# Attention scores from two float32r parts instead of three bf16 parts

## What is computed

```python
# first attention: 16 heads, 8 key heads, 32 numbers a head
q = q * cos + _rotate_half(q) * sin
k = k * cos + _rotate_half(k) * sin
att = jnp.einsum('bhqd,bhkd->bhqk', q, k) * scale
att = SOFTCAP * jnp.tanh(att / SOFTCAP)          # SOFTCAP = 50
att = jnp.where(causal[None, None], att, -jnp.inf)
att = jax.nn.softmax(att, axis=-1)
y = jnp.einsum('bhqk,bhkd->bhqd', att, v)
return y.transpose(0, 2, 1, 3).reshape(b, t, NH * HD) @ Wo
...
# second attention: 16 heads, 4 key heads, 16 numbers a head, no softcap
scores = jnp.einsum('bhqd,bhkd->bhqk', q, k) * scale
scores = jnp.where(causal[None, None], scores, jnp.finfo(scores.dtype).min)
attn = jax.nn.softmax(scores, axis=-1)
```

## Time and profile before

| | us |
|---|---|
| median of 3 runs | 3083.39 (3082.63 to 3088.0) |
| the profiled execution | 3089.23, of which the span from first to last instruction 3087.3 |
| `pa` with its norm, from the start | to 125 |
| `aa` | 125 to 453 |
| `pb` with its norm | 603 to 667 |
| `ab` | 667 to 1062 |
| PE, DVE, ACT, POOL busy over the whole span | 81%, 68%, 60%, 28% |

### The profile page before, as it was taken

How to read it: one execution, slowest core, us unless ns; L and a number is a source line. 1 busy time by engine, 2 the same in 40 slices (tenths; PEclk the granted TensorE clock), 3 DMA queues, 4 the chain that set the end, 5 groups by cost and what they waited for, 6 DMA issues and landing times. The chain is left out here.

```text
span 3087.3 us, 69834 instructions
## 1 busy us (share of the span) xinstructions
PE 2494.2 (81%) x25745; PEld 1664.7 (54%) x25832; DVE 2105.2 (68%) x4897; ACT 1849.8 (60%) x3604; POOL 873.3 (28%) x907
## 2 busy tenths in 40 slices
PE   7788877878888698577677677776999686899998
PEld 3333325643343385344444344445888565788888
DVE  7478886668787567599799899985333254666652
ACT  3388874324444443289799799993222332576678
POOL 2233334120000131255455455540000122223223
PEclk9899997878999898799999899998999776898999
DMA  3523312254233212512211222004000565522210
GB/s 123 140 47 66 70 23 91 87 108 56 45 38 42 71 52 98 108 21 29 30 16 14 30 29 29 1 1 169 1 1 1 104 137 96 127 39 33 31 41 11
DMA packets 291483, 174.00 MB, mean 56 GB/s; under 512 B 206416, under 2 KB 252512, under 8 KB 289120
## 3 DMA queue, kind: packets, MB, share of 16 engines
q1 hardware_dynamic: 282000, 161.40, 25.4%
q10 hardware_dynamic: 9168, 8.41, 1.0%
HBM read 113.84 MB, written 51.51 MB: 54 GB/s over the span
## 5 line engine op out<-in xcount | busy, mean ns | idle before, releaser
L1279 ACT ACTIVATE ad_e<-ps,ad_nm 128x1024 f32<-128x1024 f32 (+7 forms) x512 | 384.9, 760 | 96.9 <-DVE ad_nm L1340 94.9
L1340 DVE TENSOR_REDUCE ad_nm<-ps 128x1 f32<-128x1024 f32 (+7 forms) x512 | 369.2, 748 | 54.2 <-PE ps L1210 53.6
L1313 POOL TENSOR_TENSOR ad_e<-ad_e,ad_c 128x128 f32<-128x128 f32 (+7 forms) x256 | 293.6, 1147 | 15.0 <-DVE ad_rz L1353 8.2
L615 ACT ACTIVATE ab_e<-ps 128x512 f32<-128x512 f32 (+3 forms) x384 | 167.6, 490 | 204.7 <-PE ps L532 158.8
L1208 PE MATMUL ps<-ad_k_st,ad_q_st 96*128 96x512 bf16 (+3 forms) x768 | 212.8, 338 | 95.2 <-ACT ad_e L1279 47.1
L365 PE MATMUL ps<-warm,ident_b 128*128 128x512 bf16 x425 | 139.5, 394 | 114.7 <-ACT ad_prT L1264 112.7
L1364 DVE CUSTOM_DVE_ANT_0 ad_t<-ad_e,ad_rz 128x128 f32<-128x128 f32 (+7 forms) x256 | 224.0, 875 | 3.7 <-ACT ad_pr L1287 2.5
L1306 POOL TENSOR_TENSOR ad_e<-ad_e,later_k 128x128 f32<-128x128 f32 x256 | 118.9, 464 | 380.2 <-ACT ad_e L1279 380.2
L1287 ACT ACTIVATE ad_pr<-ad_t,ad_low 128x128 f32<-128x128 f32 (+7 forms) x256 | 201.0, 785 | 0.0
L1223 PE MATMUL ps<-ident,ad_pr 128*128 128x128 f32 x1152 | 174.3, 279 | 23.6 <-ACT ad_pr L1287 23.6
L1825 POOL TENSOR_TENSOR st_it_low<-st_it,st_it_high 128x256 fp32r<-128x256 f32 x128 | 98.3, 780 | 323.8 <-ACT st_it_high L2088 306.9
(11 more groups left out here) (392 smaller groups left out, 7175.0 us busy)
## 6 DMA issues: line engine op xcount, KB each, us to landing
aa_q_st<-scr_a SPq DMA_DIRECT2D x48, 256.0 KB, 5.9
split<-f_split SPq DMA_DIRECT2D x16, 768.0 KB, 3.9
ad_q_st<-scr_d SPq DMA_DIRECT2D x48, 256.0 KB, 9.7
g_w<-split SPq DMA_DIRECT2D x8, 1536.0 KB, 17.9
scr_a<-pa_parts SPq DMA_DIRECT2D x24, 384.0 KB, 2.5
scr_d<-pd_parts SPq DMA_DIRECT2D x20, 384.0 KB, 2.5
st_w_first<-split ACTq DMA_DIRECT2D x5, 1536.0 KB, 7.5
aa_k_st<-scr_a SPq DMA_DIRECT2D x48, 128.0 KB, 6.1
```

The costliest lines, as they stand in the source:

```text
L615: act.activation(e[:, u % ER, h, lo:QB], m.ps[:, n4(u, h) % 3, lo:QB], ACT.Exp, scale=scale).then_inc(s_read[0], 1)
L1279: act.activation(e[:, u % EB, s, 0:L], src, ACT.Exp, bias=nm[:, u % EB, s:s + 1], accum_out=z[:, u % EB, s:s + 1]).then_inc(exped[s], 1)
L1313: pool.tensor_tensor(e[:, k, 1, 0:L], e[:, k, 1, 0:L], c[:, k:k + 1].to_broadcast([P, L]), ALU.mult).then_inc(mixed, 1)
L1340: dve.tensor_reduce(nm[:, u % EB, s:s + 1], src, AX.X, ALU.max, negate=True).then_inc(maxed[s], 1)
```

## The change

`project_rope` gets a flag `two`, set for `pa` and `pb`. With it the parts are two float32r numbers: ACT rounds `r` (one copy), POOL subtracts (one instruction), and DVE's L278 and ACT's L309 are gone. An item's store holds 2 x 4 instead of 3 x 2 bytes a number. In `attention` three pairs (`Q_TWO`, `K_TWO`) take the place of six: 96 rows and one stack in `aa`, 48 rows in `ab`. The shift by the maximum is split in two: DVE does three instructions instead of five, SP writes two rows instead of three, and the score matmul has 50 rows. Staging a group takes seven DMAs instead of 13, in the same number of bytes; a group's rows for the maxima take six instead of 12. The memset of the ones starts at partition 32 and now covers key rows as well, so SP waits for it before it stages.

```diff
-    parts = ph.sb("parts", [P, PB, 3, QB], BF16)
+    parts = ph.sb("parts", [P, PB, 2, QB], F32R) if two else ph.sb("parts", [P, PB, 3, QB], BF16)
...
                 if n >= 2:
                     dve.wait_ge(high, n - 1)
+                    if two:
+                        dve.wait_ge(low2, n - 1)
                 dve.tensor_tensor(r[:, a, :], tc[:, a, :], ts[:, a, :], ALU.add).then_inc(summed, 1)
...
+                if two:
+                    pool.wait_ge(high, n + 1)
+                    pool.tensor_tensor(parts[:, n % PB, 1, :], r[:, a, :], parts[:, n % PB, 0, :],
+                                       ALU.subtract).then_inc(low2, 1)
+                    continue
...
+Q_TWO, K_TWO = (0, 0, 1), (0, 1, 0)
...
-    stacks = 1 if 6 * hd <= 96 else 2
-    per = 6 // stacks
+    per = len(Q_TWO)
     rows = per * hd
-    aug = 3 if plain else 0
+    aug = 2 if plain else 0
...
-    q_st = ph.sb("q_st", [rows + aug, 2, HG, stacks, T], BF16)
-    k_st = ph.sb("k_st", [rows + aug, 2, kv_in_group, stacks, T], BF16)
+    q_st = ph.sb("q_st", [rows + aug, 2, HG, T], F32R)
+    k_st = ph.sb("k_st", [rows + aug, 2, kv_in_group, T], F32R)
...
-        q_row = ph.sb("q_row", [rows, 2, HG, T], BF16)
-        k_row = ph.sb("k_row", [rows, 2, T], BF16)
+        q_row = ph.sb("q_row", [rows, 2, HG, T], F32R)
+        k_row = ph.sb("k_row", [rows, 2, T], F32R)
...
-                        for st in range(stacks):
-                            last = pe.matmul(m.ps[:, bank, lo:QB], k_st[:, par, h // share, st, kt * P:(kt + 1) * P],
-                                             q_st[:, par, h, st, qb * QB + lo:(qb + 1) * QB],
-                                             start=(st == 0), stop=(st == stacks - 1))
+                        last = pe.matmul(m.ps[:, bank, lo:QB], k_st[:, par, h // share, kt * P:(kt + 1) * P],
+                                         q_st[:, par, h, qb * QB + lo:(qb + 1) * QB], start=True, stop=True)
...
-                pool.memset(k_st[rows:rows + aug, :, :, :, :], 1.0).then_inc(ones_set, 1)
+                pool.memset(raw(k_st[32:rows + aug, :, :, :]), 1.0).then_inc(ones_set, 1)
```

More of the change, by code:

```diff
@@ L192, in norm_transpose, with project_rope @@
     ph.close()
-def project_rope(nc, m, tag, w_d, tiles, wv_d, kv, hd, vpad, cos_d, sin_d, scr, v_sb):
+def project_rope(nc, m, tag, w_d, tiles, wv_d, kv, hd, vpad, cos_d, sin_d, scr, v_sb, two=False):
     ph = Phase(nc, tag)
@@ L231, in _ @@
                 sp.dma_start(scr[:, mt * P:(mt + 1) * P, tb * QB:(tb + 1) * QB].rearrange("s p n -> p s n"),
-                             parts[:, n % PB, :, :]).then_inc(stored[n % PB], 16)
+                             parts[:, n % PB, :, :].bitcast(F32) if two else parts[:, n % PB, :, :]).then_inc(stored[n % PB], 16)
             for par in range(PB):
@@ L284, in _ @@
                 rotate(n)
-                if n >= 1:
+                if n >= 1 and not two:
                     remainder(n - 1)
                 add(n)
-            remainder(len(items) - 1)
+            if not two:
+                remainder(len(items) - 1)
         @block.gpsimd
@@ L312, in _ @@
                 first_part(n)
-                if n >= 1:
+                if n >= 1 and not two:
                     second_part(n - 1)
-            second_part(len(items) - 1)
+            if not two:
+                second_part(len(items) - 1)
             if vpad > hd:
@@ L445, in stage @@
                 tok = slice(b * T, (b + 1) * T)
-                for n in range(6):
-                    row, st = (n % per) * hd, n // per
-                    sp.dma_start(q_st[row:row + hd, par, :, st, :],
-                                 scr[Q_PARTS[n], j * HG * hd:(j + 1) * HG * hd, tok]
+                for n in range(per):
+                    row = n * hd
+                    sp.dma_start(raw(q_st[row:row + hd, par, :, :]),
+                                 scr[Q_TWO[n], j * HG * hd:(j + 1) * HG * hd, tok]
                                  .rearrange("(h d) t -> d h t", d=hd)).then_inc(staged[par], 16)
                     k0 = q_rows + j * kv_in_group * hd
-                    sp.dma_start(k_st[row:row + hd, par, :, st, :],
-                                 scr[K_PARTS[n], k0:k0 + kv_in_group * hd, tok]
+                    sp.dma_start(raw(k_st[row:row + hd, par, :, :]),
+                                 scr[K_TWO[n], k0:k0 + kv_in_group * hd, tok]
                                  .rearrange("(h d) t -> d h t", d=hd)).then_inc(staged[par], 16)
@@ L461, in stage_rows @@
                 tok = slice(b * T, (b + 1) * T)
-                for n in range(6):
-                    sp.dma_start(q_row[n * hd:(n + 1) * hd, par, :, :],
-                                 scr[Q_PARTS[n], j * HG * hd:(j + 1) * HG * hd, tok]
+                for n in range(per):
+                    sp.dma_start(raw(q_row[n * hd:(n + 1) * hd, par, :, :]),
+                                 scr[Q_TWO[n], j * HG * hd:(j + 1) * HG * hd, tok]
                                  .rearrange("(h d) t -> d h t", d=hd)).then_inc(row_staged[par], 16)
                     k0 = q_rows + j * hd
-                    sp.dma_start(k_row[n * hd:(n + 1) * hd, par, :],
-                                 scr[K_PARTS[n], k0:k0 + hd, tok]).then_inc(row_staged[par], 16)
+                    sp.dma_start(raw(k_row[n * hd:(n + 1) * hd, par, :]),
+                                 scr[K_TWO[n], k0:k0 + hd, tok]).then_inc(row_staged[par], 16)
             if plain:
@@ L478, in _ @@
                     sp.wait_ge(max_step, SPLIT * (g + 1))
-                    for s in range(3):
-                        sp.dma_start(q_st[rows + s:rows + s + 1, g % 2, :, 0, :], nmp[:, s, :]).then_inc(max_staged, 16)
+                    for s in range(aug):
+                        sp.dma_start(raw(q_st[rows + s:rows + s + 1, g % 2, :, :]), raw(nmp[:, s, :])).then_inc(max_staged, 16)
                     if g + 2 < B * GB:
@@ L689, in split_maxima @@
                 step = lambda k: wait(dve, max_step, i, 2 * SPLIT, g * SPLIT + k)
-                wait(dve, max_staged, i, 96, g * 48)
+                wait(dve, max_staged, i, 32 * aug, g * 16 * aug)
                 wait(dve, max_turned, i, 2, g + 1)
@@ L695, in split_maxima @@
                 step(3)
[L696 to L700 removed]
+                dve.tensor_tensor(nmp[:, 1, :], nmT[:], nmp[:, 0, :], ALU.subtract).then_inc(max_step, 1)
             def accrue(i, u):
@@ L2433, in attn_softcap @@
             with nc.sbuf_tensor("xnT_a", [P, KC, TOK], F32) as m.xnT:
-                project_rope(nc, m, "pa", a["wqk_a"], 6, a["wv_a"], 8, 32, 32, a["cos_a"], a["sin_a"], a["scr_a"], v_sb)
+                project_rope(nc, m, "pa", a["wqk_a"], 6, a["wv_a"], 8, 32, 32, a["cos_a"], a["sin_a"], a["scr_a"], v_sb, two=True)
             attention(nc, m, "aa", a["scr_a"], v_sb, a["wo_a"], 32, 2, 512, 256.0 ** -0.5, 50.0)
@@ L2442, in attn_plain @@
             with nc.sbuf_tensor("xnT_b", [P, KC, TOK], F32) as m.xnT:
-                project_rope(nc, m, "pb", a["wqk_b"], 3, a["wv_b"], 4, 16, 32, a["cos_b"], a["sin_b"], a["scr_b"], v_sb)
+                project_rope(nc, m, "pb", a["wqk_b"], 3, a["wv_b"], 4, 16, 32, a["cos_b"], a["sin_b"], a["scr_b"], v_sb, two=True)
             attention(nc, m, "ab", a["scr_b"], v_sb, a["wo_b"], 16, 1, 256, 0.25, None)
```

19 lines of the change are left out of this document (8 added, 11 removed).

## The result

The changed kernel takes 3464.7 us (median of 4 runs, 3461.6 to 3471.2), the kernel before 3083.7 in the same comparison. The ratio is 1.125, with a 95% interval from 1.122 to 1.128. The forecast was 3091, and the range ended at 3118.

The account below looks back on a forecast made before the run. It took `aa` as bound by ACT plus gaps, `ab` by PE's list, then DVE, and `pa` by PE. Terms -2.4 - 6 + 0 - 5 + 21 = +7.6 on 3083.4 gave 3091 us, range 3066 to 3118.

Parts of the forecast that it names:

- What bounds `ab`: In `ab`, PE's list was said to be the bound for most of the time and DVE for the rest.
- the last rival: In `ab`, float32r matmuls of 96 or 50 rows move at float32's rate: 46 us a group, about 3450 us; chance 1%.
- term 5: In `ab`, float32r weight loads cost 25 and 1 us, splitting the maxima -5: +21 us, bounds +9 and +36.
- behind 256 columns or more the load is hidden: Float32r weight loads in `ab` behind wide matmuls don't show; the 28 such matmuls a group cost 0.01 us each.
- Term 1: In `pa`'s tail, PE's wait for ACT's first copy of values goes: -2.4 us, bounds -2.4 and 0.
- Term 2: In `pb`'s tail, the same wait shrinks from 3.9 to about 1 us and the clock may hold: -6 us.
- Term 3: At the start of `aa` and `ab`, fewer DMA issues for the same bytes gain 0 us in each.
- Term 4: In `aa`, two score matmuls per head pair replace four, shortening ACT's waits: -5 us, bounds -12 and +5.
- The clock's price: In `aa`, PE sheds work and idles more, so its clock may fall for stretches: +3 us, counted within the -5.

## Why the prediction was wrong, by its steps

**What bounds `ab`** was read rightly: PE's list for most of the time, so whatever lengthens PE's work is paid. That is also why the loss is so large. At half clock PE alone sets the pace.

**The failed step** is the sentence under the last rival, "I know no reason why fewer rows should be slower", and with it term 5 as a whole. It priced the type and kept everything else, +21 us where `ab` took 394 more. But the change halves the rows of 768 row and score matmuls, and this has two prices that the sum put at nothing: the clock, and the changes of size around 512 masks. I had costed the matmuls by columns, which is right for the streaming and says nothing on the clock. The rival itself had its number near (3450) by another mechanism, a float32 rate, that no trace shows: at full clock a score matmul of 98 rows and 512 columns in float32r and the row matmul behind it start 0.23 us apart. That it came near is luck.

The 394 us can be laid out by the kernels, one step at a time. They are not independent, so another order would give other shares:

| step | `ab`, us | clock in `ab` |
|---|---|---|
| before | 391 | 0.90 |
| float32r at 96 and 98 rows, without the 9.6 us by which the zeros delay it | 424 | 0.87 |
| float32r at 48 and 50 rows, no change of size (masks of 64 rows) | 650 | 0.52 |
| float32r at 48 and 50 rows, masks of 128: the change | 785 | 0.50 |

So +33 for the type, +226 for few rows by the low clock, and +135 for the changes of size. In the other order, by the kernel with 96 and 98 rows and masks of 64 (661.6 us, 652 without the zeros), the changes of size are worth 228 us, since there they cost clock too, and the few rows the last 133. What is shown is that either alone costs more than 200 us, and both together 361.

**The row in the trace of before** that could have told me of the changes of size was there. The timeline of PE in `ab`, kernel before, has a mask 0.06 us ahead of a row matmul, with its 128 columns of weights, and one ahead of the weighing, with its 32 columns:

```profile
895.41 0.22 PE L502 MATMUL ps<-later_k,ident_b 128*128 128x128 bf16 x1
895.47 0.27 PE L499 MATMUL ps<-ab_k_row,ab_q_row 96*128 96x256 bf16 x1
...
896.04 0.22 PE L502 MATMUL ps<-later_k,ident_b 128*128 128x128 bf16 x1
896.19 0.85 PE L552 MATMUL ps<-ab_e,ab_v_st 128*32 128x384 f32 x8
```

0.15 in place of 0.06 (medians 0.149 and 0.059), and I now read the 0.09 us as the price of a change of the array's shape; no run here tests it for columns. I explained what stands around the weighing by loads that cannot run ahead, and went no further. As to the clock, the trace of before has one stretch, of 23.8 us in the linear attention, in which PE is busy 22.5 us at 0.50, with matmuls of 16 and 32 rows among ones of 128:

```profile
2593.70:2617.50 23.80, 22.53 (x368) 17.07 (x369) 10.65 (x43) 8.80 (x19) 6.55 (x5) 0.50 0.45 83
```

It shows that a busy PE can stay at half clock, and is too mixed to say why; that took the experiments.

**Term 5 as it was meant**, the price of the type, held at 98 rows for the steady groups. I said "a group should take 3 us more than its 44". From one turning of the maxima to the next it is 44.7 us before and 47.6 with 98 rows in float32r (medians of seven), 2.9 more. What the term lacked is the first group: 54.1 us from the first turning to the second, where before had 39.8, since the clock came up only at 749.9 us, 67 us after the first row matmul, and before at 716.3, 37 us after it. Those 14 us and the other groups' 14 are 28 of the 33. The parts of the price of a group were off too and made up for each other. I put the price at the load behind a mask (0.055) and at 0.01 behind a wide matmul. (The 0.055 rests on 1.07 - 0.86 - 0.17 in the prediction, which is 0.04 and not 0.05.) Measured at full clock, a mask to the next row matmul takes 0.040 (0.059 in bf16), and the price sits behind the wide float32r one: 0.324 to its mask (0.219) and 0.331 from a row matmul to another (0.220). So my "behind 256 columns or more the load is hidden" fails at these places, though not everywhere: from a score to the row matmul behind it 512 columns of float32r take 0.233, and its load begins 0.003 us after the score does. What tells the places apart is open. Timeline of PE and PEld with 98 rows; the mask's load begins with its own matmul:

```profile
901.55 0.42 PE L541 MATMUL ps<-ab_q_st,ab_k_st 98*128 98x384 f32 x1
901.81 0.10 PEld L544 LDWEIGHTS ps<-later_q,ident_b 128*128 128x128 bf16 x1
901.82 0.23 PE L544 MATMUL ps<-later_q,ident_b 128*128 128x128 bf16 x1
```

There is no change of size here, so a load that begins so late is no sure sign of one. In this kernel the loads themselves take 0.2 us, and those of bf16 0.10. Lines of weight loads with 98 rows, 760 to 1052 us:

```profile
L513 PEld LDWEIGHTS ps<-ab_k_row,ab_q_row 96*128 96x128 f32 x287 | 55.8, 201 | 21.5 <-DVE ab_nm_two L689 11.6 <-issue 2.9 <-DVE ab_nm L689 2.7
...
L544 PEld LDWEIGHTS ps<-later_q,ident_b 128*128 128x128 bf16 x206 | 20.0, 97 | 14.7 <-issue 5.7
```

**Term 1** was right: in `pa` the 64 matmuls of the values now run without the wait of the earlier trace rows, -2.9 against -2.4. **Term 2** was right on the wait and too hopeful on the clock in this profile. I said that about 1 us of the wait of the earlier trace rows stays and that the clock may fall all the same:

```profile
643.51 1.89 PE L252 MATMUL ps<-pb_wv,xnT_b 128*128 128x64 f32 x16
646.55 10.03 PE L252 MATMUL ps<-pb_wv,xnT_b 128*128 128x64 f32 x48 [1.14 <-ACT v_b L329]
```

1.14 stays, 2.8 less than the 3.94 (forecast 2.9), and 48 matmuls still take 10.03 us against 10.50, so the clock fell (at 647.1) and gave 0.5 of the 3 that I had put on it. That is -3.4 from the first record of `pb` proper; the rest of the -4.6 is the norm ahead, which the change does not touch. In four of the six profiles with this `pb` the clock fell later in these matmuls and the gain was 5.2, near the -6.

**Term 3**, nothing, held in `aa`. In `ab` the first row matmul comes 14.6 us after the stage's start, and before 12.2: 2.4 late, a little over the bound of 2.

**Term 4** was right in sign and near in size, -4 by the medians and -3.3 in this pair of profiles against -5, though the whole program's times do not tell it from noise. Gone are most of the waits of 0.45 and 0.50 of the earlier trace rows, further than to the 0.2 that I had said; the one of 1.76 before a group's last tanh, which I had left unchanged, is 1.46. But another, 0.29 before, is 1.36, just behind a stretch at half clock from 374.0 to 377.4 us. Timeline of ACT in `aa`, kernel after:

```profile
366.37 0.38 ACT L629 ACTIVATE aa_e<-ps 128x256 f32<-128x256 f32 x1 [1.46 <-PE ps L538]
...
378.47 0.38 ACT L629 ACTIVATE aa_e<-ps 128x256 f32<-128x256 f32 x1 [1.36 <-PE ps L538]
379.69 1.93 ACT L629 ACTIVATE aa_e<-ps 128x1024 f32<-128x1024 f32 x2
382.02 1.95 ACT L629 ACTIVATE aa_e<-ps 128x1024 f32<-128x1024 f32 x2
```

The clock's price was foreseen too: it falls about once a group there, every 37.5 us. `aa` took 338 us in some kernels and 347 in others, with the clock lower over the longest (0.87) than over the rest (0.90 to 0.92); that is no full account, since 0.91 goes with 337 us and with 344. `aa` keeps 96 rows in its scores and keeps most of its clock, as the row counts above would have it.

**The range** failed with the step. It was made of bounds on the terms that I had, and the price of fewer rows was not among them.

## What to carry to other kernels

Before cutting the contracted rows of a matmul, look at what it does to TensorE beyond columns: whether it goes to 64 rows or fewer beside neighbours of 128, which cost 0.10 to 0.12 us a change here, and whether PE's rows get so few that the clock stays at half, as 48 to 51 did here. Zeros are enough to keep both away: 48 rows of them took back 350 of 394 us. A busy share of 99% at a clock of 0.50 is the sign of the low clock in the profile. A short weight load that stands at "issue" until its own matmul starts is a hint of the other and no proof, since float32r showed it at 98 rows too; start times with and without padding decide.

Padding is only worth it where the narrow form brings something else. Here it didn't: at 98 rows the change is still 0.8% slower. In `ab` the zeros cost 9.6 us and the type 33, and in the profiled execution the other stages gave back 8.

## What the hardware did that I had not expected

- TensorE at 100% busy with 48-row bf16 matmuls of 512 columns ran at 0.50 of its clock for 102 us; 64, 80 and 96 rows of the same ran at 1.00. All those rows moved zeros, and so do half of those that lifted `ab` from 0.50 to 0.93: what the rows hold did not matter in these runs.
- A matmul of up to 64 rows between ones of more: 0.205 us for the two changes at full clock, 0.23 at half, in bf16 and with nothing to wait for. In `ab` in bf16 the mask's load behind a score matmul of 51 rows begins 0.534 us after its start, and behind one of 99 rows 0.002 us after.
- Stalls count for the clock. 66 rows stayed at 1.00 in pairs with 128-row masks and at 0.50 in pairs with 64-row masks, with PE shown as 100% busy in both, and 64 rows without changes of size at 1.00.
- A float32r weight load of 128 columns took 0.20 us at full clock, where bf16 took 0.10. Two row matmuls of 512 columns in float32r start 0.331 us apart, and a score and the row matmul behind it 0.233.
- Why 66 rows lose the clock part of the time in `ab` and keep it in plain pairs was not tried; the float32r loads, the weighing and the waits of `ab` were not taken apart.
